# Moving the context projection into the softmax tail, reordering the end of linear attention, and placing the first middle products behind the upper layer

## The reference

```python
x = x + attn_a(layernorm(x))   # 16 heads of 16: softmax(q k^T / 4) v, then @ Wproj.T + bproj
x = x + ffn(layernorm(x))      # h = silu(silu(x @ w1.T) @ w3.T) @ w2.T, router softmax(x @ wr.T), top 2 of 8;
                               # out.at[indices[:, k]].add(gates[:, k:k+1] * h): rows 0 to 7 alone are written
x = x + attn_b(layernorm(x))   # 16 heads of 128: causal conv of 4 taps, silu, norm of q and k,
                               # S = (1-b) S + b v k^T, o = S q, (o * silu(gate)) @ Wo
x = x + ffn(layernorm(x))
```

## Time and profile before

| | us |
|---|---|
| median of 3 runs | 1172.69 |
| lowest, highest | 1171.26, 1176.45 |
| profiled execution, time | 1177.77 |
| profiled execution, span of the core | 1176.0 |
| PE busy | 1127.3 (96%) |
| DVE busy | 932.3 (79%) |
| ACT busy | 773.7 (66%) |
| POOL busy | 635.6 (54%) |
| granted TensorE clock, mean | 0.983 |

### The profile page before, as it was taken

How to read it: one execution, slowest core, us unless ns; L and a number is a source line. 1 busy time by engine, 2 the same in 40 slices (tenths; PEclk the granted TensorE clock), 3 DMA queues, 4 the chain that set the end, 5 groups by cost and what they waited for, 6 DMA issues and landing times. The chain is left out here.

```text
span 1176.0 us, 22452 instructions
## 1 busy us (share of the span) xinstructions
PE 1127.3 (96%) x7559; PEld 907.9 (77%) x7559; DVE 932.3 (79%) x2126; ACT 773.7 (66%) x1535; POOL 635.6 (54%) x1077
## 2 busy tenths in 40 slices
PE   8999999987998899999999999999999999999788
PEld 7444434336666799999999999999999999999776
DVE  6988887836558888888888888888888888888762
ACT  3477677762447676767676777777777777676533
POOL 4020500000705777786777686777687777767630
PEclk9999999987999999999999999999999999999899
DMA  6333333300320112102111211211211211010020
GB/s 184 55 55 56 55 55 56 55 2 2 115 70 20 35 48 68 48 33 77 40 48 33 84 33 48 68 48 34 80 37 39 78 33 47 33 48 33 32 72 1
DMA packets 23449, 60.50 MB, mean 51 GB/s; under 512 B 3367, under 2 KB 8359, under 8 KB 22183
## 3 DMA queue, kind: packets, MB, share of 16 engines
q1 hardware_dynamic: 23335, 59.07, 18.8%
HBM read 44.67 MB, written 2.33 MB: 40 GB/s over the span
## 5 line engine op out<-in xcount | busy, mean ns | idle before, releaser
L1804 DVE SCALAR_TENSOR_TENSOR ln_xn<-l_proj_q,par,ln_xn 128x511 f32<-128x511 f32 (+2 forms) x192 | 142.6, 743 | 98.0 <-ACT ln_xn L1688 95.6
L698 DVE TENSOR_REDUCE a_neg_max<-a_scores 128x1 f32<-128x512 f32 x244 | 154.9, 683 | 31.2 <-PE a_scores L419 29.4
L617 ACT ACTIVATE a_probs<-a_scores_t 128x512 f32<-128x512 f32 x256 | 138.3, 600 | 59.5 <-PE a_scores_t L441 58.4
L1694 ACT ACTIVATE ln_xn<-ln_xn,par 128x512 f32<-128x512 f32 x128 | 92.6, 723 | 93.3 <-DVE ln_xn L1804 93.3
L1388 POOL TENSOR_TENSOR l_k_tok<-l_normed,k_norm 128x384 f32<-128x384 f32 x64 | 65.0, 1016 | 153.8 <-ACT l_normed L1705 151.9
L1804 DVE SCALAR_TENSOR_TENSOR ln_xn<-l_proj_k,par,ln_xn 128x511 f32<-128x511 f32 (+2 forms) x192 | 143.2, 746 | 4.5
L1705 ACT ACTIVATE l_normed<-l_turn_q,l_shift,l_scale 128x128 f32<-128x128 f32 x252 | 94.8, 457 | 22.3 <-POOL l_shift L1381 22.3
L1379 POOL TENSOR_TENSOR l_scale<-l_small,l_minus_half 128x8 f32<-128x8 f32 x64 | 105.0, 1641 | 5.0
L1705 ACT ACTIVATE l_normed<-l_turn_k,l_shift,l_scale 128x128 f32<-128x128 f32 x252 | 95.6, 480 | 0.0
L1762 ACT ACTIVATE l_gate<-l_proj_gv 128x512 f32<-128x512 f32 x64 | 38.2, 597 | 79.1 <-PE l_proj_gv L1476 79.1
L1578 PE MATMUL l_outp<-l_masked,l_values 128*128 128x128 f32 x512 | 88.6, 275 | 1.0 <-issue 1.0
(11 more groups left out here) (369 smaller groups left out, 3622.7 us busy)
## 6 DMA issues: line engine op xcount, KB each, us to landing
l_keep<-keep_rows SPq DMA_DIRECT2D x64, 448.0 KB, 3.5
a_stack<-a_dense SPq DMA_DIRECT2D x90, 128.0 KB, 4.3
head_raw<-w_heads SPq DMA_DIRECT2D x8, 1024.0 KB, 6.7
x_tok<-x SPq DMA_DIRECT2D x4, 512.0 KB, 8.3
wo_raw<-w_o SPq DMA_DIRECT2D x1, 2048.0 KB, 11.4
out<-x_tok SPq DMA_DIRECT2D x1, 1920.0 KB
a_stack<-a_max_rows_t SPq DMA_DIRECT2D x64, 4.0 KB
ctx_tok<-w_qkv SPq DMA_DIRECT2D x1, 768.0 KB, 6.8
```

The lines of the kernel that those rows point to most:

```text
L617: act.activation(probs[:, n % 2, h, :], scores_t[(4 * n + h) % TURNS][:], ACT.Exp, scale=SOFT_SCALE).then_inc(probs_done, 1)
L698: dve.tensor_reduce(neg_max[:, g % 2, at:at + 1], max_bank(g, j), AX.X, ALU.max, negate=True).then_inc(max_done, 1)
L1694: act.activation(conv[:, w, m, :], conv[:, w, m, :], ACT.Silu, bias=par[:, h, 2 * TAPS + w:2 * TAPS + w + 1]).then_inc(act_sem[w], 1)
L1804: ins = dve.scalar_tensor_tensor(conv[:, w, m, s:], proj[w][:, 0:SEQ - s], par[:, h, tap:tap + 1], conv[:, w, m, s:], ALU.mult, ALU.add)
```

## The change

It does the following.

- `project_context` is gone. Its work is eight parts (k = n // 4 is the half of the channels, n % 4 the batch). A part is `turn_part` (4 transposes), `high_part` on ACT, `low_part` on DVE, `project_part` (12 matmuls in two banks) and `add_part` on DVE (two adds). Parts 0 to 3 run in slots 64 to 68 of the softmax tail, in the bank `scores[0]` and the banks `scores[1:3]`; parts 4 to 7 follow the last head. There are 16 adds to `x_tok` instead of 8. The weight splits come in slots 60 to 63. `ln_b` steps and its POOL part are in the same block.
- `unread` matmuls are put ahead of and behind the last `context`, ahead of and among the late parts, and at the end of the block; four fillers open each FFN.
- In the FFNs batch 0's two `middle` products come right behind its second `upper`, the transposes of batch 1 between the two `upper`, and DVE does `low_parts` ahead of `normalise`. FFN d begins with (2, 1) instead of (3, 2).
- In linear attention's `drain()`: `read_state` of unit 62 comes ahead of turning back unit 63; `sum_chunks` of 62 ahead of `read_state` of 61; the keys and late queries of 62 and 63 (but for `scaled_keys` of 62) go from POOL to DVE, as does `gated_low` of 63; the output products get banks of their own (`turn_q`, `scores`, `turn_k`) for units 61 to 63; ACT's `gated_high` of 60 goes into the last step; `ln_d` has batch 0 alone.

```diff
@@ softmax_attention: PE
+            def turn_part(n):
+                k, b = n // NB, n % NB
+                if n == 0:
+                    pe.wait_ge(max_done, groups * tiles_per_group)
+                elif n < NB or n == PARTS - 1:
+                    pe.wait_ge(p_lo_done, min(n, NB))
+                else:
+                    pe.wait_ge(probs_done, 4 * groups * chunks)
+                pe.wait_ge(ctx_done, groups * quads // KD * (k + 1))
+                for t in range(TPB):
+                    last = pe.transpose(part_banks[n][:, t * P:(t + 1) * P], ctx_tok[:, b, t, k * P:(k + 1) * P], ident[:])
+                last.then_inc(p_turned, 1)
+            def project_part(n):
+                k = n // NB
+                pe.wait_ge(p_lo_done, n + 1)
+                if n == 0:
+                    pe.wait_ge(p_w_lo_done, 1)
+                for half in range(2):
+                    if n >= 1:
+                        pe.wait_ge(p_added, 2 * n - 1 + half)
+                    for e in range(2):
...
+                    last.then_inc(p_acc_done, 1)
...
+                        if last_max <= slot < last_max + NB:
+                            turn_part(slot - last_max)
...
+                        if last_max < slot <= last_max + NB:
+                            project_part(slot - last_max - 1)
+            pe.wait_ge(ctx_done, quads * groups - 1)
+            unread(misc, 4)
             context(groups * chunks - 1)
-            pe.wait_ge(ctx_done, quads * groups - 1)
+            unread(misc, 3)
             transpose_context(quads * groups - 1)
+            unread(ctx_acc, 4)
+            for n in range(NB, PARTS):
+                turn_part(n)
+            for n in range(NB, PARTS):
+                if n == PARTS - 1:
+                    ln_b.transpose(pe, 0, norm_banks)
+                project_part(n)
+                if n == NB + 1:
+                    unread(ctx_acc, 5)
+            unread(scores_t[0], 6)
@@ softmax_attention: ACT and DVE
+                if slot == last_max - 4:
...
+                    act.activation(p_w_hi, proj_w[:], ACT.Copy).then_inc(p_w_hi_done, 1)
+                if slot == last_max - 2:
+                    act.activation(w_in_hi[:], w_in_raw[:], ACT.Copy).then_inc(w_in_hi_done, 1)
+                if last_max <= slot < last_max + NB:
+                    high_part(slot - last_max)
...
+                if last_max + 2 <= slot < last_max + 2 + NB:
+                    add_part(slot - last_max - 2)
...
+            normalise(groups * quads - 1)
+            low_part(NB)
+            for n in range(NB, PARTS):
+                if n + 1 < PARTS:
+                    low_part(n + 1)
+                add_part(n)
+                if n == NB:
+                    dve.wait_ge(p_added, 2 * n + 2)
+                    ln_b.statistics(dve, 0)
+                elif n == NB + 1:
+                    ln_b.normalise(dve, 0)
+                elif n == NB + 2:
+                    dve.wait_ge(p_added, 2 * n)
+                    ln_b.statistics(dve, 1)
+            ln_b.low_parts(dve, 0, norm_banks)
@@ norm_and_ffn
+            for _ in range(4):
+                pe.matmul(up[0][:], w_in_hi[:, 0, 0:P], w_in_hi[:, :, 0:D], start=True, stop=True)
             router(0)
-            if done < 2:
-                ln.transpose(pe, 1, xt)
...
-                    for m in range(KD):
-                        upper(g, m)
+                    upper(g, 0)
+                    if g == 0 and done < 2:
+                        ln.transpose(pe, 1, xt)
+                    upper(g, 1)
+                    if g == 0 and done < 2:
+                        for n in range(2):
+                            middle(n)
...
-                if g >= 1:
+                if g >= (2 if done < 2 else 1):
...
+                if g >= done + 1 and done < 2:
+                    ln.low_parts(dve, g - 1, xt)
                 ln.normalise(dve, g)
-                if g >= done + 1:
+                if g >= done + 1 and done >= 2:
@@ linear_attention: PE, drain()
                 score_unit(LAST - 1, BODY - 2)
+                sum_chunks(LAST - 1, BODY - 2)
                 read_state(LAST - 2, BODY - 3, LAST - 4, 0)
+                wait(pe, state_done, LAST)
+                unread(chunks, 4)
+                read_state(LAST - 1, BODY - 2, 0, LAST - 1)
                 turn_back(LAST, 0)
-                sum_chunks(LAST - 1, BODY - 2)
                 turn_back(LAST, 1)
+                unread(chunks, 3)
                 score_unit(LAST, BODY - 1)
-                ln_d.transpose(pe, 0, proj)
-                read_state(LAST - 1, BODY - 2, 0, LAST - 1)
                 sum_chunks(LAST, BODY - 1)
...
-                wait(pe, added, LAST - 2)
                 project_out(LAST - 2, BODY - 3, head)
-                ln_d.transpose(pe, 1, proj)
+                ln_d.transpose(pe, 0, proj)
                 wait(pe, masked_done, UNITS)
                 project_out(LAST - 1, BODY - 2, head)
-                wait(pe, added, LAST - 1)
                 project_out(LAST, BODY - 1, head)
+                unread(chunks, 4)
@@ linear_attention: DVE, drain()
                 token_statistics(LAST, BODY - 1)
+                shifted_keys(LAST - 1)
+                decayed_keys(LAST - 1)
+                decayed_queries(LAST - 1, BODY - 2)
+                mask(LAST - 1, BODY - 2)
+                carry(LAST - 1, BODY - 2)
+                decays(LAST, BODY - 1, 16 * NB * PAIRS)
+                gate_out(LAST - 2, BODY - 3)
+                add_out(LAST - 4, BODY - 5)
                 wait(dve, added, UNITS - BODY + 2)
                 ln_d.statistics(dve, 0)
+                scaled_keys(LAST)
+                shifted_keys(LAST)
+                decayed_keys(LAST)
                 ln_d.normalise(dve, 0)
                 mask(LAST, BODY - 1)
+                decayed_queries(LAST, BODY - 1)
                 gate_out(LAST - 1, BODY - 2)
+                carry(LAST, BODY - 1)
+                gate_out(LAST, BODY - 1)
+                add_out(LAST - 3, BODY - 4)
+                gated_low(LAST, BODY - 1)
+                add_out(LAST - 2, BODY - 3)
                 wait(dve, added, UNITS - BODY + 4)
                 ln_d.statistics(dve, 1)
                 ln_d.low_parts(dve, 0, proj)
                 add_out(LAST - 1, BODY - 2)
                 add_out(LAST, BODY - 1)
@@ build
-        norm_and_ffn(nc, semaphore, "d", ffn, ..., ln_d, (NB - 1, NB - 2), out=out)
+        norm_and_ffn(nc, semaphore, "d", ffn, ..., ln_d, (2, 1), out=out)
```

More of the change, by code:

```diff
@@ L869, in _ @@
+                if slot == last_max - 3:
+                    dve.wait_ge(p_w_hi_done, 1)
+                    dve.tensor_tensor(p_w_lo, proj_w[:], f32(p_w_hi), ALU.subtract).then_inc(p_w_lo_done, 1)
+                if slot == last_max - 1:
                     dve.wait_ge(w_in_hi_done, 1)
                     dve.tensor_tensor(w_in_lo[:], w_in_raw[:], f32(w_in_hi[:]), ALU.subtract).then_inc(w_in_lo_done, 1)
-                    ln.normalise(dve, 0)
-                elif b == 2:
-                    dve.wait_ge(added, 4)
-                    ln.statistics(dve, 1)
@@ L875, in _ @@
-            ln.low_parts(dve, 0, turned[0])
+                if last_max <= slot < last_max + NB:
+                    low_part(slot - last_max)
+            normalise(groups * quads - 1)
+            low_part(NB)
+            for n in range(NB, PARTS):
+                if n + 1 < PARTS:
[9 more added lines that the diff above has]
+                    ln_b.statistics(dve, 1)
@@ L1057, in copy_logits, with middle_silu @@
                 act.activation(logit_rows[:, g % 2, :], rows, ACT.Copy).then_inc(router_read, 1)
+            def middle_silu(n):
+                act.wait_ge(mid_done, n + 1)
+                act.activation(hidden[:, 2 * n:2 * n + 2, :], mid[n % 2][:], ACT.Silu).then_inc(mid_read, 1)
             copy_logits(0)
-            if done < 2:
-                ln.high_parts(act, 1, xt)
             for g in range(NB + 1):
@@ L1067, in _ @@
                                        ACT.Silu).then_inc(up_read, 1)
+                        if g == 0 and m == 0 and done < 2:
+                            ln.high_parts(act, 1, xt)
+                    if g == 0 and done < 2:
+                        for n in range(2):
+                            middle_silu(n)
                     if g + 1 < NB:
@@ L1648, in step, with unread @@
                     project_out(v, (k - 5) % BODY, 2 * (pair if k >= 5 else pair - 1))
+            def unread(bank, count):
+                for _ in range(count):
+                    pe.matmul(bank[:], wo_hi[:, 0, 0:P], wo_hi[:, 0:2, :], start=True, stop=True)
             def drain():
```

206 lines of the change are left out of this document (83 added, 123 removed).

## The result

The kernel after takes 1169.59 us (median of 20 runs, 1167.85 to 1171.36), the kernel before, run beside it, 1173.47 us (20 runs, 1171.13 to 1179.90). The ratio is 0.9968, 95% interval 0.9958 to 0.9978: 3.8 us faster, where 11.8 were forecast. The interval leaves out 1, so there is a gain, but it is a small one, and 1169.6 lies above the upper end of the range, 1168.0.

What follows compares the result with a forecast made beforehand. TensorE at full clock bounds most of the span, except two seams at lower clock and chains at linear attention's end. Terms -6.1-1.0-7.4+2.7 = -11.8 us, taken from median 1172.7, give 1160.9 us; range 1154.5 to 1168.0.

Steps and rivals of the forecast that it cites:

- The base: Whole kernel: the -11.8 us costed on the profiled execution (1177.8) applied unchanged to the median 1172.7, giving 1160.9.
- A: Softmax tail and projection: four projection parts moved into the tail, next stage at 286.8 for 292.93, -6.1 us.
- the walk: Slot-by-slot timing of the new softmax tail and projection at full clock: last division 270.5, next stage 286.8.
- rival (5): Tail's end shifts by what the parts save, and linear attention's end stays as long: 1174 us; chance 0.03.
- Rival (1): The clock falls in the softmax tail all the same: A = +2, total -3.7, 1169 us; chance 0.10.
- So the four parts cost nothing there: Softmax tail: 7.8 us of parts leave its end at 270.5 for 270.62, if the clock stays up.
- Rival (2): Tail bound by PE, only a third of the parts hidden: A = -0.9, total -6.6, 1166 us; chance 0.12.
- B: First FFN: waits removed, middles moved, four fillers added; between -1.9 and 0, taken as -1.0 us.
- POOL's weight split starts 3 us later and ended 8 us ahead of the stage's end: nothing: First FFN: the later weight split on POOL was claimed to cost nothing.
- C: End of linear attention: PE's waits shortened, -8.9 us by the walk less 1.5 for the SBUF port, -7.4.
- the 1.5: End of linear attention: loss of 1.5 us in all where moved DVE steps meet POOL at the SBUF port.
- D: Last FFN: one batch normalised ahead instead of two, with transposes, fillers and a wait uncovered on PE, +2.7 us.

Runs made afterwards that it cites:

- before, again: The kernel before, unchanged, profiled and timed anew: median 1174.07 us, ratio 1.000; its second profiled execution took 1173.43 us.
- a_alone: The kernel before with only the new softmax stage and projection, both FFNs and linear attention old: 1172.97 us, ratio 0.9983 to before.
- +3.0 alone: The kernel before with only the new first FFN (order and fillers): 1175.81 us, ratio 1.0026 to before.
- end_fill: The kernel after, POOL's head-weight split ahead of its memset, eight unread matmuls behind the first FFN's last middle: 1163.47 us, ratio 0.9923 to before.
- no_fill: The kernel after without any of its new unread matmuls (tail, both FFNs, drain): 1165.94 us, ratio 0.9948 to before.

## Why the prediction was wrong

The forecast was -11.8 us from 1177.8 and the same difference from 1172.7. The measured time is 8.7 us above 1160.9. The sum on the profiles is -8.1 in place of -11.8, which makes 3.7; the other 5.0 are the base: 5.1 was taken off for the median, and the profiled execution of after lies 0.1 above it.

**The base ("the same difference gives 1160.9").** This step failed first. The profiled execution of before lay 4.3 us above the median of 20 runs, that of after 0.1 above. The prediction's second largest gain, A, was costed against a tail at half clock, which about one execution in ten has. The numbers at hand hinted at it: three runs within 1171.3 to 1176.5 and the profiled one above all three; and the earlier trace rows has the context matmuls at both clocks (1.06 and 1.93 us). The 14.9 us from the second scores of slot 67 to the end of the tail are 10.3 at full clock (255.56 to 265.82 in before, again). Taken off 292.93, these 4.6 leave 288.3 to the walk's 286.8: A = -1.5 and not -6.1. The mechanism was the forecast's own rival (5), first half: the parts in the tail shift its end by what they save. Rival (1) gives 1169, next to the measured 1169.6, by luck: its condition, the lower clock in the tail all the same, did not come (1.00).

**A: -6.1, measured -6.5 on the two profiles, -0.2 against before, again, -2.0 in the medians.** The walk was right: last division 270.95 (270.5 expected), first router's stage 286.41 (286.8), clock 1.00 over 256 to 276, context matmuls 1.06. So -6.1 is met on the two profiles because the one it was taken from had the half clock. "So the four parts cost nothing there" is wrong at equal clock: they cost 5.1 us of 7.8, and the projection behind is 5.35 shorter (15.46 for 20.81). Rival (2), a third hidden, is the measured share; it too was priced against the half clock. Of the 2.0 in the medians 0.6 is the clock at the start of the first FFN, by the profile of `a_alone`; what makes up the rest isn't shown.

**B: -1.0, measured +0.6 (0.0 against before, again), +3.0 alone.** PE's own part was right: from first to last matmul 37.97 us for 39.18, -1.2; the waits of 1.62 and 0.3 are gone, the new one for the silu is 0.69 (0.8 expected), and the first 4 us have 1.00. The step that failed is "POOL's weight split starts 3 us later and ended 8 us ahead of the stage's end: nothing". It looked at the end of the stage, not at what DVE does beside the split. Counted from the stage's first matmul, `wo_lo` starts at 26.0 us for 22.7, the comparison at 28.8 for 30.0; so they meet for 6.2 us where they had met for 1.7. The Trainium skill, SBUF — State Buffer, section "SBUF: two separate sides", calls the shared pair an exclusive lock for the whole instruction. The 6.35, 4.67 and 1.19 us beside one, one earlier and eight POOL instructions agree. The prediction weighed that rule for C and left it out for B.

**Linear attention's body: 0, measured +2.3 (768.35 for 766.09; +1.6 against before, again).** It was not in the sum. The idle time of PE ahead of it grew to 4.29 us, and the clock of 1.2 GHz reached into its first 6 us, and again at 32 us. In the profile of `end_fill`, with 1.37 us idle, neither is there and the body takes 763.61.

**C: -7.4, measured -7.2.** The drain takes 26.68 us for 33.92. PE's waits are 0.47, 0.15, 0.59, 0.18, 0.57 and 1.25; only the last, for the state's sum on DVE, is over the 1 us expected. The port took 1.0 of the 1.5: normalise is 2.35 us beside `gated_low` for 1.37 alone, the key steps on DVE 0.54 to 0.61. A scan on DVE at the drain's start (1096.60, beside another `gated_low`) took 2.11 us for 1.36 and is not in that 1.0. Counted from the first turning, the last add comes 7.2 us earlier, but it starts at 1122.69, not at 1118, since less had been gained ahead of it. The clock stayed at 1.00, as in all nine profiles with the new drain; in all five with the old one it falls. By `no_fill` the fillers weren't needed for it: the shorter waits are what is left as the reason, which is argued and not shown.

**D: +2.7, measured +2.8**, 37.6 us from the first matmul to the gates' wait (37 expected). It was costed with no cover, and there was none.

Left open: what makes the later fall in linear attention, how often the fall at its start comes in each kernel, and how much of the medians' scatter is the drain's clock (0.59 and 0.63 in the two profiles of before).

## What to carry to other kernels

Before a gain is costed against a profile, put its time beside the other runs: where it lies above all of them and a seam shows the lower clock, walk the kernel before at full clock too, and cost the change against both. When two engines' work slides along each other, look at every long instruction of the one (8.92 us here) and every dependent step of the other beside it, not at whether the long one is through by the stage's end; cut it in pieces or start it earlier. Work moved into an engine's gaps costs what the gaps don't hold (over half of it here). Unread matmuls cost their time in every execution to save some in a few: with all of the change's taken out the median was 2 to 4 us lower, though the intervals overlap. And where executions differ by their clock, one profile of each kernel doesn't compare two kernels: put the mean clocks of all the runs beside them.

## What the runs showed of the hardware that was not expected

- The same program with the same idle pattern in the tail ran at 1.00 in one execution and 0.50 in another (3.03 and 3.04 us of 4 busy ahead of it), which is 4.8 us of the tail in a spread of 8.8 (1171.1 to 1179.9). The Trainium skill, TensorE: Matmul & The Clock Gate, "Part 1: The HAM clock gate (the "warmup" mystery)", says that the watch on PE's activity is free-running and doesn't start anew with the kernel; the two executions agree with it, without proving it. After the change, with PE busy 19.69 of 20 us, the spread of the runs is 3.5 us.
- A 128x128 comparison on DVE stood still for 6.06 of its 6.35 us behind one POOL instruction of 8.92 us. Beside eight of about 1.3 us the steps with two inputs took 0.93 to 1.27 us, and a reduction with one input its 0.29.
- The first 6 us of linear attention, full work on PE, ran at 0.58 behind 4.29 us of idle time (after), behind the same 2.49 us at 0.73 (before) and at 1.00 (before, again), and at 1.00 in all three profiles with 1.37 us.
